# TensorE's program written out for all 32 pairs, in a four-engine kernel whose engines each run a loop over pairs

## The reference, cut to what matters

```python
# token part
h = layernorm(x.reshape(b, t, 192)); h = relu(conv2d(h, conv1_w)); h = layernorm(h)
h = relu(conv2d(h, conv2_w)); h = layernorm(h); h = relu(conv2d(h, conv3_w))
res = layernorm(concat(h[:, :t], h[:, t:], axis=2)); h = res @ out_w + out_b
# attention: scores by L1 distance, for each of 8 heads and 64 columns
a[b, s, t, h] = -sum_w |q[b, s, h, w] - k[b, t, h, w]| / 8        # k = x * wk
a = softmax(concat([a, 0], axis=1), axis=1)[:, :t]
o = (einsum('bsdh,bshw->bdhw', a, vf) + einsum('bdsh,bshw->bdhw', a, vb)).sum(heads)
h = h + x + gelu_like(o) @ fanin_w.T
# one expert per token
h = h + relu(relu(xf @ W1[argmax]) @ W2[argmax])
```

## Time and profile before

| | us |
|---|---|
| median of 3 runs | 3506.68 (3501.89 to 3508.08) |
| the profiled execution | 3508.91 |
| its span, first to last instruction | 3507.0 |
| mean granted TensorE clock, as a share of full | 0.986 |

### The profile page before, as it was taken

How to read it: one execution, slowest core, us unless ns; L and a number is a source line. 1 busy time by engine, 2 the same in 40 slices (tenths; PEclk the granted TensorE clock), 3 DMA queues, 4 the chain that set the end, 5 groups by cost and what they waited for, 6 DMA issues and landing times. The chain is left out here.

```text
span 3507.0 us, 78749 instructions
## 1 busy us (share of the span) xinstructions
PE 3243.3 (92%) x23140; PEld 2458.9 (70%) x23140; DVE 3086.9 (88%) x4389; ACT 2723.1 (78%) x4859; POOL 2856.5 (81%) x2792
## 2 busy tenths in 40 slices
PE   8899999999999999999999999999999999999888
PEld 6676777776777777677767777766777777777555
DVE  5888889998898989988999889989989999989886
ACT  3777787887787877877788878778778788777875
POOL 2888888888888888888888888878888888888885
PEclk8999999999999999999999999999999999999999
DMA  6778777787787787777888877877777887778884
GB/s 135 154 153 164 155 155 153 157 162 156 151 163 154 157 161 158 158 150 153 161 160 159 160 153 156 164 149 157 157 155 157 166 159 157 154 158 160 163 159 86
DMA packets 199653, 543.63 MB, mean 155 GB/s; under 512 B 69142, under 2 KB 133398, under 8 KB 146744
## 3 DMA queue, kind: packets, MB, share of 16 engines
q0 software_dynamic: 73728, 501.51, 72.0%
q1 hardware_dynamic: 125880, 41.54, 5.9%
HBM read 10.93 MB, written 2.10 MB: 4 GB/s over the span
## 5 line engine op out<-in xcount | busy, mean ns | idle before, releaser
L925 DVE TENSOR_REDUCE S<-psU 128x16 f32<-128x1024 f32 x2183 | 2604.4, 1217 | 297.8 <-PE psU L486 281.3
L486 PE MATMUL psU<-flat,kT 99*128 99x256 bf16 x16384 | 2304.1, 275 | 212.5 <-ACT absd L711 102.9
L711 ACT ACTIVATE absd<-psU 128x1024 f32<-128x1024 f32 x1913 | 1936.7, 1023 | 554.3 <-PE psU L486 541.0
L486 PEld LDWEIGHTS psU<-flat,kT 99*128 99x128 bf16 x16384 | 1495.6, 98 | 855.2 <-DVE S L925 219.3
L1194 POOL TENSOR_TENSOR absd<-absd 128x1024 f32<-128x1024 f32 (+2 forms) x512 | 1179.8, 2304 | 248.9 <-DMA absd<-absd 245.0
L1198 POOL TENSOR_TENSOR absd<-absd 128x512 f32<-128x512 f32 (+2 forms) x512 | 610.3, 1192 | 40.2
L1183 POOL DMA_DIRECT2D absd<-absd x512 | 454.2, 887 | 200.4 <-ACT absd L711 145.2
L1201 POOL TENSOR_TENSOR absd<-absd 128x256 f32<-128x256 f32 (+2 forms) x512 | 351.7, 687 | 40.1
L498 PE MATMUL psC<-c1in,w 128*128 128x384 f32 (+1 forms) x930 | 309.4, 415 | 0.8 <-DVE c1in L969 0.8
L590 PE MATMUL psZ<-P,v 128*128 128x256 f32 x1024 | 288.6, 384 | 0.0
L517 PE MATMUL psC<-c3in,w 128*128 128x128 f32 x1240 | 251.8, 287 | 1.7 <-DVE c3in L969 1.7
(11 more groups left out here) (180 smaller groups left out, 2231.3 us busy)
## 6 DMA issues: line engine op xcount, KB each, us to landing
absd<-absd POOLq DMA_DIRECT2D x412, 1024.0 KB, 7.9
absd<-absd POOLq DMA_DIRECT2D x65, 768.0 KB, 6.5
flat<-qparts SPq DMA_DIRECT2D x3072, 8.0 KB, 4.1
absd<-absd POOLq DMA_DIRECT2D x35, 512.0 KB, 4.9
xin<-in_x SPq DMA_DIRECT2D x32, 192.0 KB, 8.0
flat<-pattern SPq DMA_DIRECT2D x4, 768.0 KB, 10.9
out_h<-result SPq DMA_DIRECT2D x32, 64.0 KB, 6.0
w<-in_w SPq DMA_DIRECT2D x1, 1280.0 KB
```

The costliest lines, as they stand in the source:

```text
L486: mm = nc.tensor.matmul(psU[:, slot % PLACES, m], kT[0:ROWS + 3, b, m, :], flat[0:ROWS + 3, half % HALVES, :, lo:lo + BLOCK], start=True, ...
L711: nc.scalar.activation(absd[:, c % GROUPS, :, u], psU[:, slot % PLACES].rearrange("p (n a) s w -> p n (a s w)", n=2), ACT.Abs).then_inc(a_ ...
L925: nc.vector.tensor_reduce(S[:, b, hd, SB * c:SB * c + SB], psU[:, slot % PLACES].rearrange("p a s w -> p s a w"), AX.XY, ALU.add, apply_ab ...
```

## The change

`program` takes a new argument `looped`. Where it is false, pairs 1 to 29 are emitted one after the other with `i` as a Python number, in place of one body inside a hardware loop. TensorE's program alone is called so. The order of all instructions that compute, on every engine, and the meaning of all waits stay; in TensorE's stream the values waited for are now constants.

```diff
-        def program(eng, prologue, iteration, epilogue):
+        def program(eng, prologue, iteration, epilogue, looped=True):
 
             prologue()
             iteration(0, late=False)
-            with eng.Fori(1, PAIRS - 2) as i:
-                iteration(i)
+            if looped:
+                with eng.Fori(1, PAIRS - 2) as i:
+                    iteration(i)
+            else:
+                for i in range(1, PAIRS - 2):
+                    iteration(i)
             iteration(PAIRS - 2, tokens=False)
             iteration(PAIRS - 1, tokens=False, ahead=False)
             epilogue()
...
-            program(pe, prologue, iteration, epilogue)
+            program(pe, prologue, iteration, epilogue, looped=False)
```

## The result

The written-out kernel takes 3567.95 us in the median (3549.27 to 3572.57), the kernel before 3507.38 (3501.89 to 3514.65) on the same chip: 1.0169 times as long, with an interval of 1.0149 to 1.0190, or 60.6 us more. The direction was predicted. The size was not: 3521 was forecast, and 3540 was the upper end of the range.

What follows compares the result with a forecast made beforehand. TensorE was taken to set the pace, with some 6 us idle per 105.6 us pair waiting for consumers. Terms 0 + 0 + 10 - 1 + 5 = +14 us gave 3523, predicted median 3521, range 3500 to 3540.

Steps and rivals of the forecast that it cites:

- the form of the waits: TensorE's late waits ahead of units: 0.09 us more each, four per pair pass it on, +10 us, ends 0 and 26.
- The loop's edge: TensorE's branch and register instruction between looped pairs: removed, hidden behind the consumer, worth 0, at most 7.5 us gain.
- Register instructions: On TensorE's sequencer in looped pairs: removed, run while matmuls work, worth 0, with an unsupported bound of 64 us.
- The small jobs: TensorE's small jobs with two waits, the first late: reordering helps about three per pair, at most 8 us gain, taken as -1.
- Instruction fetches: Queue q8: 28 more pairs bring about 160 packets of 16 KB, 0.2 us a pair, +5 us, ends 0 and 25.
- The clock: Falls of 4.4 us each at a few of 29 pairs; two more or fewer are 9 us either way.
- Clearly slower: Rival: packets delay query rows or absd additions about once a pair, 25 us, waits at upper end; 3530 to 3560, chance 0.14.
- All cover holds: Rival: every late TensorE wait is absorbed and packets land beside other traffic; 3506 to 3512 us, chance 0.23.
- faster: Rival: TensorE's loop has a hidden cost, its edge of 7.5 us or fetches of 26 more; 3475 to 3500, chance 0.11.
- GpSimd's waits for `absd`: Sign on GpSimd: the fetch term is wrong if these waits grow by more than a few us per pair.
- Pairs at full clock: Sign that the prediction is right: written-out pairs without a fall of the clock take 106.0 to 106.7 us.

Runs made afterwards that it cites:

- experiment 3: Written-out kernel with ACT's normalisation moved from slot 6 to slot 14: 3540.95 us, 1.0102 times the kernel before.
- experiment 4: Looped kernel before with ACT's normalisation moved from slot 6 to slot 14: 3498.23 us, 0.9978 times the kernel before.
- experiment 6: Written-out kernel with the normalisation at slot 14 and the wait for the psU place back on the weight load: 3528.89 us, 1.0060 times before.
- experiment 2: Kernel before with TensorE's loop body covering two pairs instead of one, waits in looped form: 3694.4 us, 1.0535 times before.
- experiment 1: Written-out kernel with query-row waits moved behind the wait for the psU place, which rides on the weight load again: 3551.65 us, 1.0147 times before.
- experiment 5: Kernel before with TensorE's pairs 1 to 14 kept in the loop and 15 to 29 written out: 3541.48 us, 1.0106 times before.
- experiment 7: Looped kernel before with SyncE issuing six more 16 KB HBM-to-HBM copies per pair that nobody reads: 3541.93 us, 1.0106 times before.
- experiment 8: Looped kernel before with GpSimd's rstd norm step moved from slot 4 to slot 6, no packets added: 3633.67 us, 1.0367 times before.

## Why the prediction was wrong, point by point

Three differences between the ratios divide the 60.6 us, each taken against the kernel before on the same chip:

| what | from | us |
|---|---|---|
| GpSimd's lateness, slot 11 and the clock | after 60.6, less experiments 3 and 4: 35.6 + 7.1 | 18 |
| the form of the waits | experiments 3 and 6: 35.6 - 21.7 | 14 |
| packets ahead of query rows, with the clock level | experiments 6 and 4: 21.7 + 7.1 | 29 |

The intervals of these ratios reach some 5 to 7 us to either side, so a difference of two is uncertain by some 8 us, and the first line, made of three, by more. It is the loosest for another reason too: the parts don't simply add. In the profiled execution of after, 10 more falls at slot 11 than before, at 4.4 us each, are 44 us, but taking them away gave back only 18 us over what the same edit gave the loop. Waits for query rows rose from 22.1 us in after to 34.6 us in experiment 3, since slack that a slow or waiting TensorE leaves is gone. The lines are shares in this order of removal; another order would give the clock more and the query rows less.

- **The loop's edge, 0: right as read.** A branch of 208 ns hid behind a consumer. It was right because one pair's body stays on the engine; experiment 2 shows 4.3 to 7.2 us where it doesn't.
- **Register instructions, 0: nothing speaks against it.** Pairs without a fall got longer by 0.77 us, not shorter, with all of these gone.
- **The form of the waits, 10: right.** The 28 semaphore instructions per pair are there:

```profile
L487 PEldq EVENT_SEMAPHORE  x28: 51/51/51, 1476.9 to 1577.3; - x28
```

and at slot 56 of pair 13 of after, in order of time, DVE ends at 1518.73 + 1.22 = 1519.95 and the unit starts at 1520.10, 0.15 us later, where the earlier trace rows had 0.05:

```profile
1518.73 1.22 DVE L929 TENSOR_REDUCE S<-psU 128x16 f32<-128x1024 f32 x1
...
1520.10 0.60 PE L490 MATMUL psU<-flat,kT 99*128 99x256 bf16 x4
```

  Twice, by experiments 1 and 6, it measured 14 us, which the uncertainty doesn't tell from the 10 forecast.
- **The small jobs, -1:** too small to be seen in any run.
- **Instruction fetches, 5: the step that failed.** The count held (187, where about 185 was forecast). The price was read from pair 1 against pair 14: one has packets, both have a fall, and they differ by 0.2 us. That comparison can't give the price. Pair 14 has no packet, but GpSimd was late in it for another reason: TensorE idled 1.77 us at slot 11, and the clock fell. Pair 1 had the same through a packet (2.27 us of idle time; one closing packet of group 13 started at -2.54, the others by -3.97). I had compared a pair that already paid with another that already paid; against pairs 10 or 15 the reading would have been 4.7 to 5.3 us, an upper end of 28 x 5.3 = 148 us that the range never had. It also used a pair of one kind of coincidence for 29 that each meet the packets elsewhere. Measured, by the table above: 29 us through query rows, and 18 us through slot 11 and the clock, against the 5 of the sum and the 25 of its upper end.
- **The clock, 9 us either way: the other part of the same failure.** I took falls as events that come at a few pairs. They aren't: before, 4 of the 5 pairs with over 1.1 us of idle time at slot 11 fell there and none of the 24 others; after, 14 of 15 and none of 14. That could be read in before alone, since in order of time pair 14 differs from pair 10 at slot 11 and nowhere earlier on TensorE:

```profile
1560.21 0.88 POOL L1183 DMA_DIRECT2D absd<-absd  x1 [1.47 <-ACT absd L711]
...
1566.29 0.77 ACT L760 ACTIVATE x<-h,nmrn,rstdn 128x64 f32<-128x64 f32 x2 [1.37 <-POOL nmrn L1222]
...
1568.02 0.57 PE L486 MATMUL psU<-flat,kT 99*128 99x256 bf16 x2 [1.77 <-ACT absd L711]
```

  A term with a price of 4.4 us and a cause belongs in the sum, and its count must be asked for each change to the timing ahead of its place.
- **The rivals.** "Clearly slower" named the mechanism, its two victims and the point from which it decides, a transfer's slack. It was given 0.14 and 0.9 us a pair. The 0.9 us is what a packet occupies; what it does to a transfer that is about to land was up to 2.5 us in the table above, and what a late landing starts on GpSimd and in the clock comes on top. "All cover holds" and "faster" fell with every written-out kernel: the fastest of them, experiment 6, is at 1.0060 (1.0046 to 1.0074).
- **What was to be seen.** GpSimd's waits for `absd` growing by more than a few us per pair was my sign that the fetch term is wrong. They grew by 53.6 us in all, 1.7 us a pair, and the term was wrong nevertheless: 2.5 us in one group of sixteen were enough. Pairs at full clock were to be 106.0 to 106.7 and came at 106.88.

**What stays open.** That one large packet holds up one part of sixteen of an addition is seen in the DMA records (the closing packets above), and the falls come with the packets in the two halves of experiment 5 and in experiment 2. It was not produced in isolation, since the copies of experiment 7 were cut up. Why the landing follows the last closing packet by 1.1 us in pair 6 and by 0.37 in pair 18 isn't known, nor which of the 16 DMA engines carries the packets. Pair 14 of before had GpSimd late without any: its issue for group 15 stood idle for 1.47 us, ended by a copy of ACT's, and what made it do so only there wasn't found.

## What to carry to other kernels

In this kernel a loop whose body stays on the engine cost nothing at an edge that a consumer hides, while writing it out put a steady stream of instruction packets among transfers that land just in time. Price such packets by the slack of the transfers they meet, not by their own length. When two stretches are compared to price an effect, first ask whether both already pay for something else. Where falls of the clock come at a fixed place, find the idle time ahead of it and give the engine that feeds it slack: here one number, the slot of a normalisation, took away all four falls at that place and made the looped kernel 7 us faster.

## What the runs showed of the hardware that was not expected

- One idle stretch of TensorE of over 2 us at slot 11 was followed by a fall to 1.2 GHz in 47 of 47 pairs, and one of under 0.7 us in 1 of 153. The fall mostly lasted 10.2 us. In experiment 8, the idle time and the fall together made a pair some 4.9 us longer (111.0 against 106.1).
- An instruction packet of 1.33 us that started 4.1 us ahead of a pair came with a landing 2.5 us later: one of the addition's 16 closing packets started as it ended, 1.8 us behind the others. One that started 4.3 us ahead, with all 16 gone, moved nothing.
- A taken branch of TensorE took 0.21 us where a pair's body was held, and 4.3 to 7.2 us where a body of two pairs was not.
- A copy of one 16 KB row was moved in pieces of 1 KB, while an instruction packet of 16 KB went whole.
